# Mean stage of a graph network: sums and deviations of the node rows in PSUM, and rows made zero before they are stored

## The reference

```python
x = layernorm(x + L0(x, ...))                    # attention per channel; rows without an edge: layernorm(x)
# L1
summed = segment_sum(x[src], dst, num_segments=n)
agg = summed / maximum(deg, 1)[:, None]
h = agg @ W_l + x @ W_r + b
mu = mean(h, axis=0); var = mean(square(h - mu), axis=0)      # over all 100000 nodes
h = relu((h - mu) * rsqrt(var + 1e-5) * gamma + beta)
x = layernorm(x + h / norm(h))
```

## Time and profile before

| | |
|---|---|
| median of 3 runs | 3195.01 us (3185.26 to 3198.27) |
| profiled execution, its own time | 3199.08 us |
| its span | 3197.4 us |
| mean granted clock of TensorE | 0.864 |
| mean stage, first to last instruction | 833.0 to 1147.4 us |
| busy in the whole span | PE 79%, DVE 73%, POOL 59%, ACT 56% |

### The profile page before, as it was taken

The page is one execution under the profiler, slowest core; times in us unless marked ns, Lnnn a source line. Parts: engine busy times, 40 slices in busy tenths (PEclk is TensorE's granted clock), DMA queues, the critical chain, the costliest instruction groups (busy, mean ns, idle before and its releaser), DMA issues. The chain is left out here.

```text
span 3197.4 us, 54660 instructions
## 1 busy us (share of the span) xinstructions
PE 2520.5 (79%) x14271; PEld 1719.4 (54%) x14271; DVE 2339.4 (73%) x4347; ACT 1800.0 (56%) x4100; POOL 1887.6 (59%) x1934
## 2 busy tenths in 40 slices
PE   3986777787568779969984769997999799986662
PEld 1554555555457667745543546665666566653331
DVE  5467888888778758859985857775344388889995
ACT  3695666666322248848771236663333377777773
POOL 4755777700488810038882048885787678846666
PEclk9798777777788888869995989997999899999995
DMA  3242444433466668833321756564555433333331
GB/s 91 71 114 80 121 116 116 116 100 97 122 197 200 185 140 179 176 94 114 104 87 49 171 153 172 165 171 134 134 139 139 115 112 112 110 94 96 90 89 37
DMA packets 745066, 391.68 MB, mean 122 GB/s; under 512 B 518724, under 2 KB 650799, under 8 KB 744944
## 3 DMA queue, kind: packets, MB, share of 16 engines
q1 hardware_dynamic: 693756, 332.28, 38.0%
q0 software_dynamic: 51200, 58.03, 7.2%
HBM read 215.54 MB, written 175.61 MB: 122 GB/s over the span
## 5 line engine op out<-in xcount | busy, mean ns | idle before, releaser
L1354 POOL DMA_INDIRECT g_W<-t,g_cols x400 | 461.1, 1153 | 116.8 <-issue 100.9
L467 POOL DMA_INDIRECT fr_W<-in_x,fr_idx x400 | 413.4, 1033 | 173.7 <-issue 114.9
L1354 POOL DMA_INDIRECT me_W<-t,me_cols x200 | 237.9, 1190 | 58.0 <-issue 49.0
L3165 POOL DMA_INDIRECT out<-ou_F,ou_ways x200 | 209.7, 1048 | 75.6 <-issue 51.2
L1354 POOL DMA_INDIRECT ou_W<-t,ou_cols x200 | 219.8, 1099 | 58.1 <-issue 43.0
L3592 POOL DMA_INDIRECT de_V<-t,de_cols x200 | 217.2, 1086 | 53.0 <-issue 41.1
L1344 POOL COPY de_cols<-pos 128x8 int32 (+1 forms) x25 | 7.0, 278 | 265.6 <-POOLq L88 265.5
L1344 POOL COPY g_cols<-pos 128x8 int32 (+1 forms) x50 | 38.3, 767 | 188.5 <-POOLq L88 188.3
L1065 PE MATMUL at_pL<-at_XF,w_logit 128*128 128x512 f32 x100 | 90.0, 1055 | 63.4 <-ACT at_XF L1120 63.4
L939 ACT ACTIVATE me_nzt<-me_pXT 128x512 f32<-128x512 f32 x47 | 28.1, 598 | 171.9 <-PE me_pXT L922 171.9
L1344 POOL COPY me_cols<-pos 128x8 int32 (+1 forms) x25 | 5.3, 211 | 195.8 <-POOLq L88 195.7
(11 more groups left out here) (639 smaller groups left out, 8500.2 us busy)
## 6 DMA issues: line engine op xcount, KB each, us to landing
mg_y<-wanted SPq DMA_DIRECT2D x50, 256.0 KB
at_nx<-in_x SPq DMA_DIRECT2D x50, 256.0 KB
x<-at_nz SPq DMA_DIRECT2D x50, 256.0 KB, 3.3
x1T<-at_nzt SPq DMA_DIRECT2D x50, 256.0 KB, 2.5
t<-up_X SPq DMA_DIRECT2D x100, 128.0 KB
t<-g_HS SPq DMA_DIRECT2D x50, 256.0 KB
t<-g_HD SPq DMA_DIRECT2D x50, 256.0 KB
g_D<-t SPq DMA_DIRECT2D x50, 256.0 KB
```

Source lines behind the costliest of these rows:

```text
L467: self.nc.gpsimd.indirect_dma_start(out=self.W[w][b][:, (2 * t + h) * C:(2 * t + h + 1) * C], out_offset=None, in_=self.table, in_offset=b ...
L1354: nc.gpsimd.indirect_dma_start(out=slot(w, b, t), out_offset=None, in_=table, in_offset=bass.IndirectOffsetOnAxis(ap=cols[w][:, c:c + 1], ...
L3165: nc.gpsimd.indirect_dma_start(out=out, out_offset=bass.IndirectOffsetOnAxis(ap=ways[w][:, c:c + 1], axis=0), in_=F[w][b][:, t * C:(t + 1) ...
```

## The change

In the mean stage the lane's sums and inverse deviations lie in PSUM (two small tiles, one bank each) instead of in SBUF; the attention stage keeps them in SBUF. So L866 and L900 write PSUM and L871 and L910 have one operand there and the other in SBUF. As both halves b share a bank, `act_dev` waits for earlier norms and `dve_norm` for both deviations.

The rows that end no run are made zero where they arise. In the attention stage the 128 x 4 deviations `zt[:, 2]` are multiplied by `last` before Z is multiplied by them. In the mean stage a table `rmean = rcount x last` is made once and the mean is taken with it. X has a column of ones every 129 columns, and PE takes the moments straight from X; the copy XM, its semaphore and its multiplication are gone. SP's load of `d1` rows waits for PE's moments of X instead of DVE's masked copy, PE waits for the mean and the landing of the `d1` rows, and DVE's mean waits for the moments of two steps before.

```diff
 class NodeLane:
+        self.sums = [s[:, 0, :] for s in self.st]
+        self.devs = [s[:, 2, :] for s in self.st]
+        if in_psum:
+            sums, devs = g.ps("nsum", [P, 2, NODE_ROWS]), g.ps("ndev", [P, 2, NODE_ROWS])
+            self.sums = [sums[:, b, :] for b in range(2)]
+            self.devs = [devs[:, b, :] for b in range(2)]
...
     # dve_center: reduce writes self.sums[b], scalar_tensor_tensor reads over(self.sums[b], C)
     # act_dev
+            if self.in_psum:
+                reuse(act, d["norm"], 2 * i)
-            s.activation(self.st[b][0:p, 2, :], self.st[b][0:p, 1, :], ACT.Exp, scale=-0.5)
+            s.activation(self.devs[b][0:p, :], self.st[b][0:p, 1, :], ACT.Exp, scale=-0.5)
     # dve_norm
-            dve.wait_ge(d["dev"], last_of(i, b))
+            dve.wait_ge(d["dev"], last_of(i, 1 if self.in_psum else b))
...
 attention_stage, DVE
                     for b in second:
                         dve.wait_ge(e["zdev"], last_of(r, b))
+                        v.tensor_tensor(zt[b][:, 2, :], zt[b][:, 2, :], k.last[:, bass.ds((2 * r + b) * CT, CT)],
+                                        ALU.mult).then_inc(e["zmasked"], 1)
+                    for b in second:
+                        dve.wait_ge(e["zmasked"], last_of(r, b))
                         v.tensor_tensor(groups(Z[b][:, :], CT), groups(Z[b][:, :], CT), over(zt[b][:, 2, :], C), ...
...
 mean_stage
-        X = both("X", [P, CE])
+        X = both("X", [P, CT * (P + 1)])
+        rmean = g.sb("rmean", [P, NT])
-        XM = pairs("XM", [P, CT * (P + 1)])
-        lane = NodeLane(nc, g, k, a["x"], first, count)
+        lane = NodeLane(nc, g, k, a["x"], first, count, in_psum=True)
 # SP, own_rows
-                            sp.wait_ge(e["masked"], 2 * q + (b - 3))
+                            sp.wait_ge(e["gram"], 2 * q + (b - 2))
 # PE, moments
-                        pe.wait_ge(e["masked"], last_of(q, b))
+                        pe.wait_ge(e["mean"], last_of(q, b))
+                        pe.wait_ge(d1_in[w][b], ring_count(q, w, 16))
-                            m = XM[b][:, n * (P + 1):(n + 1) * (P + 1)]
+                            m = X[w][b][:, n * (P + 1):(n + 1) * (P + 1)]
 # DVE, ahead of the loop
-                for b in range(2):
-                    v.memset(XM[b][:, :], 1.0).then_inc(e["starts"], 1)
+                for w in range(2):
+                    for b in range(2):
+                        v.memset(groups(X[w][b][:, :], CT)[:, :, P:P + 1], 1.0).then_inc(e["starts"], 1)
+                v.tensor_tensor(rmean[:, :], k.rcount[:, :], k.last[:, :], ALU.mult).then_inc(e["starts"], 1)
 # DVE, mean
+                            dve.wait_ge(e["gram"], 2 * q + (b - 2))
-                        v.tensor_tensor(ends(X[w][b])[:, :, 1, :], ..., over(k.rcount[...], C), ALU.mult)
+                        v.tensor_tensor(mean(X[w][b][:, :]), ..., over(rmean[...], C), ALU.mult)
-                    for b in range(2):
-                        dve.wait_ge(e["mean"], last_of(q, b))
-                        dve.wait_ge(d1_in[w][b], ring_count(q, w, 16))
-                        dve.wait_ge(e["gram"], 2 * q + 1)
-                        v.tensor_tensor(groups(XM[b][:, :], CT)[:, :, 0:P], groups(X[w][b][:, :], CT),
-                                        over(k.last[...], P), ALU.mult).then_inc(e["masked"], 1)
```

More of the change, by code:

```diff
@@ L807, with __init__ @@
 class NodeLane:
-    def __init__(self, nc, g, k, x, first, count):
-        self.nc, self.k, self.x, self.first, self.count = nc, k, x, first, count
+    def __init__(self, nc, g, k, x, first, count, in_psum=False):
+        self.nc, self.k, self.x, self.first, self.count, self.in_psum = nc, k, x, first, count, in_psum
         F = NODE_ROWS * C
@@ L865, in dve_center @@
             dve.wait_ge(self.x_in[w][b], 8 * i + (8 if w else 16))
-            v.tensor_reduce(out=self.st[b][0:p, 0, :], in_=groups(self.X[w][b][0:p, :], G), op=ALU.add, axis=AX)\
+            v.tensor_reduce(out=self.sums[b][0:p, :], in_=groups(self.X[w][b][0:p, :], G), op=ALU.add, axis=AX)\
                 .then_inc(d["sum"], 1)
@@ L870, in dve_center @@
             dve.wait_ge(d["sum"], last_of(i, b))
-            v.scalar_tensor_tensor(groups(self.X[w][b][0:p, :], G), over(self.st[b][0:p, 0, :], C), -1.0 / C,
+            v.scalar_tensor_tensor(groups(self.X[w][b][0:p, :], G), over(self.sums[b][0:p, :], C), -1.0 / C,
                                    groups(self.X[w][b][0:p, :], G), ALU.mult, ALU.add).then_inc(d["cen"], 1)
@@ L899, in act_dev @@
             act.wait_ge(d["ln"], last_of(i, b))
-            s.activation(self.st[b][0:p, 2, :], self.st[b][0:p, 1, :], ACT.Exp, scale=-0.5).then_inc(d["dev"], 1)
+            if self.in_psum:
+                reuse(act, d["norm"], 2 * i)
+            s.activation(self.devs[b][0:p, :], self.st[b][0:p, 1, :], ACT.Exp, scale=-0.5).then_inc(d["dev"], 1)
     def dve_norm(self, dve, i, w):
@@ L1803, in mean_stage @@
         count = NODE_PAIRS - first
-        lane = NodeLane(nc, g, k, a["x"], first, count)
+        lane = NodeLane(nc, g, k, a["x"], first, count, in_psum=True)
+        own = lambda ap: groups(ap, CT)[:, :, 0:C]
+        mean = lambda ap: groups(ap, CT)[:, :, C:P]
         got, d1_in, agg_out = ([g.pair(f"{n}{w}_") for w in range(2)] for n in ("got", "d1_in", "agg_out"))
@@ L1807, in mean_stage @@
         ones_z = g.sem("ones_z"); lowered = g.sem("lowered")
-        e = {n: g.sem(n) for n in ("starts", "turned", "summed", "back", "mean", "masked", "gram")}
+        e = {n: g.sem(n) for n in ("starts", "turned", "summed", "back", "mean", "gram")}
         assert count == ITERS - 1
@@ L1838, in own_rows @@
                         if again(q):
-                            sp.wait_ge(e["masked"], 2 * q + (b - 3))
-                        sp.dma_start(ends(X[w][b])[:, :, 0, :], one(by_chunk(k.d1), 2 * q + b)).then_inc(d1_in[w][b], 16)
+                            sp.wait_ge(e["gram"], 2 * q + (b - 2))
+                        sp.dma_start(own(X[w][b][:, :]), one(by_chunk(k.d1), 2 * q + b)).then_inc(d1_in[w][b], 16)
                 def step(q, r, w):
@@ L1848, in step @@
                         sp.wait_ge(e["mean"], last_of(q, b))
-                        sp.dma_start(one(by_chunk(k.agg), 2 * q + b), ends(X[w][b])[:, :, 1, :])\
+                        sp.dma_start(one(by_chunk(k.agg), 2 * q + b), mean(X[w][b][:, :]))\
                             .then_inc(agg_out[w][b], 16)
@@ L1867, in _ @@
                 t = nc.tensor
-                pe.wait_ge(e["starts"], 4)
+                pe.wait_ge(e["starts"], 7)
                 pe.wait_ge(ones_z, 2)
@@ L1926, in _ @@
                 dve.wait_ge(ones_z, 2)
+                dve.wait_ge(e["starts"], 7)
                 dve.wait_ge(e["gram"], 1)
@@ L1946, in step @@
                             dve.wait_ge(agg_out[w][b], ring_count(q, w, 16) - 16)
-                        v.tensor_tensor(ends(X[w][b])[:, :, 1, :], groups(pB[b][:, :], CT),
-                                        over(k.rcount[:, bass.ds((2 * q + b) * CT, CT)], C), ALU.mult)\
+                            dve.wait_ge(e["gram"], 2 * q + (b - 2))
+                        v.tensor_tensor(mean(X[w][b][:, :]), groups(pB[b][:, :], CT),
+                                        over(rmean[:, bass.ds((2 * q + b) * CT, CT)], C), ALU.mult)\
                             .then_inc(e["mean"], 1)
-                    for b in range(2):
-                        dve.wait_ge(e["mean"], last_of(q, b))
-                        dve.wait_ge(d1_in[w][b], ring_count(q, w, 16))
-                        dve.wait_ge(e["gram"], 2 * q + 1)
-                        v.tensor_tensor(groups(XM[b][:, :], CT)[:, :, 0:P], groups(X[w][b][:, :], CT),
-                                        over(k.last[:, bass.ds((2 * q + b) * CT, CT)], P), ALU.mult)\
-                            .then_inc(e["masked"], 1)
                 by_node_step(dve, step)
```

4 lines of the change are left out of this document (2 added, 2 removed).

## The result

The changed kernel takes 3145.58 us (median of 4 executions, 3140.28 to 3156.10) against 3190.14 us for the kernel before (four executions, 3168.43 to 3198.27). The ratio is 0.9859, with a 95% interval of 0.9819 to 0.9899: faster by 45 us, 32 to 58. Two more comparisons of the same two kernels gave 0.9853 (0.9802 to 0.9904) and 0.9858 (0.9812 to 0.9903).

What follows compares the result with a forecast made beforehand. POOL's queue of 200 gathers was taken to bound the mean stage. Holds -37.3, stage end +1, attention +1 gave -35.3 us, from a median of 3195.0 to about 3160 us, range 3149 to 3178.

Steps and rivals of the forecast that it cites:

- What bounds the stage, and the hold: Mean stage: POOL's 200 gathers set its length; those beginning under DVE instructions with two SBUF inputs are held until these end.
- The size of that term: Mean stage: time the gathers lose to holds, 37.2 us by one count and 37.4 by another, taken as 37.3.
- All of it comes back: Mean stage: nothing else, PE or DVE, is slower than 10.52 us a step, so no loss is counted for the loop.
- DVE reading PSUM at 0 cost: Mean stage: a PSUM operand costs DVE 0; the bound at half speed was 2.7 us a step.
- SP's queue at 0: Mean stage: d1 load waits 1 to 4 us longer, for PE's moments; cost 0, up to 1 us a step if PE is late.
- The end of the mean stage, +1: End of the mean stage: PE may finish a little later behind the last gather than now, 1 us.
- The attention stage, +1: Attention stage: new products take 0.34 us a step, mostly covered by DVE's wait for ACT; 1 us, or 8.5 without cover.
- The sum: Whole kernel: -37.3 + 1 + 1 = -35.3 us, from the median of 3195.0 to 3159.7, rounded to 3160.
- The third rival: Mean stage: gathers are held all the same; only about 5.6 us under L1954 returns, time 3190 to 3198 us; chance 0.05.
- The chances: Whole kernel: faster (below 3179 us) 0.91, same 0.06, slower 0.03.
- PE's takeover: Mean stage: at a low clock PE's step tends to 11.6 us, time about 3187 or 3175; chance 0.14 for 3170 to 3179.
- a slow broadcast from PSUM: Mean stage: DVE reads the broadcast at about a quarter speed, 15 us a step, time 3250 us; chance 0.03.

Runs made afterwards that it cites:

- e7: Changed kernel plus an unread 128 x 512 product twice a step where the masked copy stood, both inputs in SBUF: mean-stage gathers 266.9 us, ratio 0.9855 to before.
- e8: Changed kernel plus the same unread 128 x 512 product twice a step, one input in PSUM: mean-stage gathers 261.0 us, ratio 0.9835 to before.
- e4: Kernel before plus only the attention stage's two small mask products per step, masked copy kept: mean-stage gathers 293.6 us, ratio 0.9966.
- e11: Kernel before plus the attention stage's two small products per step, multiplying by ones instead of the mask: mean-stage gathers 300.0 us, ratio 0.9957.
- e13: Kernel before plus one 128 x 4 fill at the head of DVE's mean-stage program: second gcn stage's gathers 277.7 us (283.3 before), ratio 0.9982.
- e3: Changed kernel with sums and deviations back in SBUF, masked copy still gone: mean-stage gathers 272.0 us, ratio 0.9884 to before.
- e6: Kernel before with only the masked copy's mask read from PSUM: mean-stage gathers 277.1 us, ratio 0.9900.
- e14: Kernel before plus one 128 x 4 fill in DVE's output-stage program, behind the second gcn stage: that stage's gathers 282.8 us, ratio 0.9975.

## Why the prediction was wrong, and what of it was right

*What bounds the stage, and the hold.* Right, and now shown: e7 against e8 changes one operand's memory and turns the holds on and off. The Trainium skill's rule in SBUF — State Buffer, "Who interferes with whom", that a DVE instruction with two SBUF inputs contends with GpSimd's reads, agrees with this pair (gathers up to 1.53 us in e7, up to 1.03 in e8). The inference beside it, that making descriptors isn't held up by a `tensor_tensor`, can't be used for such a gather, which is held. Whether the hold is on its reading of the indices or on the descriptors is not shown.

*The size of that term.* -37.3 forecast; measured 38.3 in the first pair of profiles, 33.3 to 39.5 over all pairs of three and three, 37.0 between the means. Right. Its words that a gather is held until the instruction ends leave out the 0.87 us that follow.

*All of it comes back.* Right. PE at a clock of 0.86 kept up with 10.52 us a step, and waited 52.2 us for rows.

*DVE reading PSUM at 0 cost.* Right: 682 and 681 ns.

*SP's queue at 0.* Right for the path, and the wait was where the text put it: SP now waits 28.6 us for PE's moments (1.4 for the copy before), node rows come later, DVE waits 8.8 us for them in ten places, and POOL never noticed. In the view of waits on the DMA queue of SP, after (sum, count, longest, in us):

```profile
SPq L1863 <- DVE me_X L1966: 75.3, 22, 13.2
SPq L1854 <- PE me_pG L1913: 28.6, 31, 2.9
```

*The end of the mean stage, +1.* Wrong by a little. From the end of the last gather to the start of the stage's last instruction it was 12.0 us in the profile before and 8.7 after; other profiles of before have 8.9 and 10.4, of after 8.6 and 9.6. On average that is 1.5 us less, not 1 more, but it goes with the granted clock and not clearly with the edit: the mean clock there was 0.60, 1.00 and 0.85 in the three of before and 1.00, 1.00 and 0.97 in those of after. Where both were at 1.00, it is 8.9 against 8.7 and 8.6. The last moments take 1.95 us after, where they took 2.72, in the timeline after:

```profile
1102.22 1.95 PE L1913 MATMUL me_pG<-me_X 128*128 128x129 f32 x16
```

*The attention stage, +1.* The new product puts 0.19 us on DVE's way in a step, not 0.34, and L1224's slack takes all of it in the one kind of step and 0.11 in the other. The stage is 0.9 us longer in the mean of three profiles, 576.7 against 575.9 up to the next stage, and not longer in e4 and e11 (575.1, 575.6). Right.

*The sum.* This is the step that failed. It has no term for the stages that aren't edited and takes them as unchanged, without a reason. The second gcn stage takes 5.6 us less, and the profiles of e13 and of the other edited kernels show that this comes with any edit ahead of it. The mean stage's 38.5 us (means of three profiles, up to the next stage) and these 5.6 are 44, beside the 45 measured. The second fault is the level: 3195.0 was the median of three executions, and four later medians are 3187.8 to 3193.5, so the forecast stood some 5 us too high from the start (4.9 against the 3190.1 of this comparison), and the range left only 11 us below it, too little for both. Added up: 5.6 for the second gcn stage, 4.9 for the level and 2.2 for the mean stage (38.5 in place of 37.3 - 1, mostly the clock at its end) are 12.7 of the 14.4. The rest is within the spread: the other unedited stages move by several us from profile to profile. That the sum comes so close is in part luck, as the mean stage's own difference runs from 33 to 42 us over the pairs of profiles.

*The third rival.* It said that if only the copy's hold went, 5.6 us would come back. e3 and e6 gave 27 and 22. The text added up the holds by the instruction under which each gather began, as if they were independent, and they aren't. It did not decide the forecast, since all of them went, but for half of the change the forecast would have been wrong by some 20 us.

*The chances.* Faster had 0.91 and was right. The range 3149 to 3178 missed 3145.6. No run supports PE's takeover or a slow broadcast from PSUM.

Still open: what an edit's place shifts in the second gcn stage; why e4 and e11 gain 11 and 14 us in the whole while e13 gains 6 and e14 8, or nothing, within about 10 us either way; why, of two gathers that begin 0.07 us into L871, one is held for one instruction (1.48 us) and one for four (3.29); and why a few that begin shortly ahead of such an instruction are caught by it.

## What to carry to other kernels

When a queue of indirect gathers sets a stage's length, look at the gathers' maximum beside their median, and at what DVE runs where the long ones begin; putting one small broadcast operand in PSUM costs DVE nothing and took all the holds away here. Don't share such a loss out among the instructions by adding up rows: one hold sets up the next, so that removing either cause alone gave back 27 to 33 of 38 us. And take the level from more than three executions, and leave room for a few us in stages that an edit only shifts: here a fill of 128 x 4 in an earlier stage moved one stage's gathers by 5.6.

## What the runs showed of the hardware

- A gather's issue is held under a DVE `tensor_tensor` or `scalar_tensor_tensor` with two SBUF inputs until that instruction's end or that of a later one in the row, and then takes another 0.86 to 0.90 us (483 gathers in thirteen profiles, up to 3.29 us in all); not at all with one input in PSUM (200 gathers between 0.99 and 1.03 us, 23 of them begun under such a product in e8).
- Under a scan with two SBUF inputs it is held too, and ends 0.80 to 0.81 us after the scan (second gcn stage, 26 gathers over 1.06 us in the profile before); in the mean stage, where the scan has one input in PSUM, none of those that begin under it is over 1.03 us.
- DVE read a stride-0 broadcast from PSUM at the speed of one from SBUF (682 against 683 ns for 128 x 512), and ACT's Exp on 128 x 8 took 173 ns into PSUM and 204 into SBUF.
- A store and load whose 64-column pieces lie 129 columns apart in SBUF, with a DMA share of 0.77, cost the path nothing.
- The 200 gathers of the unedited second gcn stage repeated to 0.3 us over three profiles of the kernel before (283.3 to 283.6) and to 0.7 over three of the changed one (277.5 to 278.2), and changed by 5.6 with a fill of 128 x 4 ahead of them. The 200 of the first gcn stage do not repeat like that: 329.1 to 333.3 in the same three profiles of before.
